# Reordering the matmuls of the last FFN: second products 0 and 1 side by side, wide products 2 and 3 side by side, the output product ahead of the low-rank product

## What is computed

```python
def _L1_ffn_ref(x, U1, V1, b1, U2, V2, b2):      # D_MODEL, D_FF, RANK = 256, 1024, 64
    P = jnp.einsum('bsd,dr->bsr', x, U1)
    H = jax.nn.gelu(jnp.einsum('bsr,rf->bsf', P, V1) + b1)
    Q = jnp.einsum('bsf,fr->bsr', H, U2)
    return jnp.einsum('bsr,rd->bsd', Q, V2) + b2
...
x = x + jnp.tanh(g_ffn[1]) * _L1_ffn_ref(_layernorm(x, axis=-1), ...)
```

## Time and profile before

| | |
|---|---|
| runs before (3) | 698.24, 698.32, 700.71 us, median 698.32 us |
| profiled execution | 698.65 us |
| its span, from first to last instruction | 696.5 us |
| PE busy | 658.6 us (95%) |
| ACT, DVE, POOL busy | 451.7, 427.9, 201.9 us |
| mean granted clock of TensorE | 0.993 |
| bodies of stage d | about 603 to 692 us of the span |

### The profile page before, as it was taken

One profiled execution on the slowest core, in us unless ns is written; L12 is line 12 of the kernel. 1 busy time (PEld: TensorE's weight loads), 2 busy tenths in 40 slices (PEclk: granted clock), 3 DMA queues, 4 the chain that ended last, 5 costly groups with the idle time before them and its releaser, 6 DMA issues.

```text
span 696.5 us, 11909 instructions
## 1 busy us (share of the span) xinstructions
PE 658.6 (95%) x3653; PEld 457.5 (66%) x3653; DVE 427.9 (61%) x981; ACT 451.7 (65%) x1204; POOL 201.9 (29%) x299
## 2 busy tenths in 40 slices
PE   5799899999999999799999999999999998799997
PEld 3565555555544457688888887888888875556654
DVE  7854757776775647566767576566665685343522
ACT  7656655535545543667887787778778877646452
POOL 6565423310110003224432342333223230142110
PEclk9999999999999999999999999999999999999999
DMA  8731116601000005434344443433444331001112
GB/s 280 224 106 61 51 41 233 106 1 61 1 0 1 0 1 123 93 95 101 93 115 123 124 104 88 116 95 93 117 122 121 92 69 25 2 1 61 43 50 90
DMA packets 45809, 57.90 MB, mean 83 GB/s; under 512 B 13152, under 2 KB 24258, under 8 KB 45634
## 3 DMA queue, kind: packets, MB, share of 16 engines
q1 hardware_dynamic: 45762, 57.33, 30.5%
HBM read 27.46 MB, written 4.19 MB: 45 GB/s over the span
## 4 chain that ended last, share of the span: by engine, by line
PE 82%; SPq 5%; ACT 3%; DVE 3%; issue 2%; POOL 2%; DMA 2%; DVEq 0%; POOLq 0%; ACTq 0%
PE bank L1191 12%; PE bank L1493 7%; PE bank L1405 7%; PE bank L1423 6%; PE bank L1203 6%; PE bank L1446 5%; PE bank L1469 4%; PE bank L1636 4%; PE bank L1486 4%; SPq L531 4%; PE bank L1432 4%; PE bank L1167 3%; PE bank L1626 3%; PE bank L1171 2%; PE bank L1627 2%
## 5 line engine op out<-in xcount | busy, mean ns | idle before, releaser
L970 ACT ACTIVATE c_junk<-bank,c_nmx 128x256 bf16<-128x256 f32 x256 | 116.3, 469 | 9.3 <-DVE c_nmx L1961 9.2
L1961 DVE TENSOR_REDUCE c_nmx<-bank 128x4 f32<-128x1024 f32 x64 | 75.3, 1219 | 34.8 <-PE bank L1446 34.8
L1191 PE MATMUL bank<-b_o,cw 128*128 128x512 f32 x192 | 90.8, 603 | 0.2 <-ACT b_o L827 0.2
L803 ACT ACTIVATE b_h<-bank,cb 128x512 f32<-128x512 f32 x48 | 32.8, 686 | 51.2 <-PE bank L1191 51.2
L1090 ACT ACTIVATE d_h<-bank,b_col 128x512 f32<-128x512 f32 x64 | 39.6, 686 | 39.4 <-PE bank L1627 39.4
L992 ACT ACTIVATE c_pT<-bank 128x1024 f32<-128x1024 f32 x64 | 62.0, 1017 | 4.8 <-PE bank L1469 3.7
L1405 PE MATMUL bank<-c_ctxT,wsrcT 128*128 128x256 f32 x256 | 61.8, 386 | 0.0
L1191 PEld LDWEIGHTS bank<-b_o,cw 128*128 128x128 f32 x192 | 34.2, 190 | 41.3 <-issue 39.2
L1423 PE MATMUL bank<-wsrcT,c_ctxT 128*128 128x256 f32 x240 | 56.7, 379 | 0.0
L1469 PE MATMUL bank<-c_stack 99*128 99x256 f32 x256 | 46.7, 315 | 6.6 <-DMA c_stack<-c_rows 6.4
L1405 PEld LDWEIGHTS bank<-c_ctxT,wsrcT 128*128 128x128 f32 x256 | 48.3, 193 | 6.3
(11 more groups left out here) (202 smaller groups left out, 1384.2 us busy)
## 6 DMA issues: line engine op xcount, KB each, us to landing
c_stack<-c_parts SPq DMA_DIRECT2D x192, 128.0 KB
a_ctx<-in_ctx SPq DMA_DIRECT2D x16, 512.0 KB, 4.0
c_ctx<-in_ctx SPq DMA_DIRECT2D x16, 512.0 KB, 3.3
out_x<-x_sb SPq DMA_DIRECT2D x7, 512.0 KB, 2.9
x_sb<-in_x SPq DMA_DIRECT2D x3, 1024.0 KB, 10.2
mask_b<-in_mask_BxS_fk SPq DMA_DIRECT2D x1, 2048.0 KB, 12.8
x_sb<-in_x SPq DMA_DIRECT2D x2, 512.0 KB, 5.5
wsrc_raw<-in_L_xattn_W_src SPq DMA_DIRECT2D x1, 1024.0 KB, 7.3
```

The lines of the kernel that those rows point to most:

```text
L970: op = nc.scalar.activation(c_junk[:, tc, j, :], scores(tc)[:, j, :], ACT.Exp, bias=c_nmx[hg][:, tc, j:j + 1], accum_out=c_sum[hg][:, tc, ...
L1191: op = mm(bank[2 * u + h][:], cw1[:, c, h * P:(h + 1) * P], b_o[n % LANES][:, c, :], start=c == 0, stop=c == DK - 1)
L1961: v.tensor_reduce(c_nmx[hg][:, tc, :], scores(tc), AXIS.X, ALU.max, negate=True)\
```

## The change

On PE, `body_d` runs `second_d(n, 1)` right after `second_d(n, 0)`, so that `hidden_d(n, 2)` and `hidden_d(n, 3)` stand together, and `out_d(n - 1)` stands ahead of `lowrank_d(n + LEAD)`. `out_d` gets one more wait, for the copies of the turned group out of bank 5, which it overwrites. No other engine's program changes, and no instruction is added or taken away.

```diff
@@ out_d
                 need(pe, d_q_ok, n + 1)
+                need(pe, d_xT_ok, 2 * min(n + LEAD + 2, NG))
                 need(pe, d_y_ok, 2 * n)
@@ body_d
                 second_d(n, 0)
+                second_d(n, 1)
                 hidden_d(n, 2)
-                second_d(n, 1)
                 hidden_d(n, 3)
+                if n > 0:
+                    out_d(n - 1, 1 - n % 2)
                 if n + LEAD < NG:
                     lowrank_d(n + LEAD)
-                if n > 0:
-                    out_d(n - 1, 1 - n % 2)
                 second_d(n, 2)
                 second_d(n, 3)
```

## The result

| | before | changed |
|---|---|---|
| median of 20 runs | 698.44 us | 700.83 us |
| lowest and highest | 695.72, 701.48 | 698.32, 703.67 |
| ratio | | 1.0028, 95% interval 1.0015 to 1.0041 |
| turn of body 0 to last output product, from the traces | 85.99 us | 88.12 us |

The change makes the kernel 0.28% slower. The last row of the table isolates the changed part: it is the distance between two starts on PE, the turn of body 0 (605.27 before, 608.54 after) and the output product of group 7 (691.26 and 696.66). It grew by 2.13 us; 0.28% of 698.44 is 2.0 us.

What follows compares the result with a forecast made beforehand. PE, 82% of the chain, bounds the kernel, with DVE's equal 6.00 us path next. Late turns add 2.35 us by body 6, bodies 6 and 7 return 0.28: 698.32 + 2.07 = 700.4 us, range 698.2 to 702.3.

Steps and rivals of the forecast that it cites:

- The price of a form: PE, stage d: entering second products costs 0.14 us, wide products 0.21, once per run; grouping saves 0.35 per body.
- Rival 2: Stage d on PE: form price is paid per half product, so bodies take 12.37 us, about +4.6, 702.9 us; chance 0.06.
- DVE's 6.00 us stay, PE's cover shrinks to 4.79: Low-rank product to next turn: PE stands idle 1.21 us, body 12.02 us against 11.31, 0.71 more.
- Rival 1: Stage d: DVE's path has unseen slack, so the forms' gain comes through; body 10.81 us, 695.5 us; chance 0.08.
- Body 0 gives nothing: Body 0 saves 0.35 us, but POOL's bias additions hold DVE's normalization, so body 1's turn stays at 616.61.
- Rival 3: Body 1: normalization gets ahead of POOL's last addition, turn about 1.3 us earlier; +0.8, 699.1 us; chance 0.06.
- Bodies 6 and 7: No turn there and second 1 waits for the gelu: 9.64 us instead of 9.78, gain 0.14 each, 0.28 together.
- The two paths are equal: Kernel before, low-rank product to next turn: DVE needs 6.00 us and PE has 6.00 us of work.
- The new wait at nothing: Output product's wait for the turned group's copies: taken at nothing, at most 0.06 us in each of 7 places, 0.4 in all.
- The clock unchanged by the idle time: Bodies 2 to 5: granted clock stays 1.00 although PE stands idle 1.2 us in each.

Runs made afterwards that it cites:

- e4: Changed kernel with the low-rank product ahead of the output product again, leaving only the grouping: body 10.93 us, ratio 0.9953 to the kernel before.
- e7: Kernel before with second 0 and 1 and wide 2 and 3 grouped, no swap, DVE normalizing one body earlier: body 10.80 us, ratio 0.9946.
- e3: Changed kernel with DVE normalizing each group one body earlier: body 10.65 us, ratio 0.9909 to the kernel before.
- e1: Changed kernel with DVE taking in the output product before splitting the low-rank product: body 11.11 us, ratio 0.9959 to the kernel before.
- e2: Kernel before, PE untouched, with DVE normalizing each group one body earlier: body 11.16 us, ratio 0.9946 to the kernel before.
- e6: Kernel before with only the output product's new wait added: body 11.31 us, ratio 1.0015 (0.9993 to 1.0037).

## Why the prediction was right

It said 700.4 us and +0.3% (+2.07 us); measured were 700.83 and +0.28%, and +2.13 us in stage d. The near match of the last two is in part luck: from the turn of body 1 to the start of body 6 the loss was 2.25 us instead of 2.35, and bodies 6 and 7 gave back some 0.14 in all instead of 0.28. The two misses cancel; the mechanism does not hang on either.

- The price of a form (0.14 and 0.21 on entering, paid once for a run): right. Second 0 and 1 take 1.88, wide 2 and 3 take 2.03, and e4 gives 0.38 per body where 0.35 was worked out, e7 against e3 0.15 where 0.14 was. Rival 2 (the price is paid per product) is refuted by these. Second products 2 and 3 pay the 0.14 behind the output product too (1.88 for 16), where both sides are fp32 and only the form changes. At the wide products form and precision change together, so what the 0.21 is paid for was not separated.
- DVE's 6.00 us stay, PE's cover shrinks to 4.79: right. The idle time ahead of the turn is 1.15 and the body 12.00 (12.02). e1 and e3 show the cause: both change DVE alone and take the loss away. Rival 1 (slack in the chain) is refuted, since there is no gap between the steps, and its figure of 10.8 us per body needs the chain to be moved, as e3 does.
- Body 0 gives nothing, because of POOL: right, 11.36 us against 11.34. Rival 3 (the normalization gets ahead of POOL's last addition) did not happen: the third addition starts at 616.31 and DVE comes to the normalization at 616.80. That the normalization is held up by POOL was read from its length in every profile, not tried with POOL's additions moved.
- Bodies 6 and 7: the mechanism was right, the size was not. The term was 0.14 us for each; from second 0 to second 0 the changed kernel takes 9.71 us (679.19 to 688.90), against 9.77 before (673.67 to 683.44), a gain of 0.06. The run of second products, with a wait in its middle, took 2.17 us (679.19 to 681.36), close to the upper of the two bounds given (1.14 + 1.01 = 2.15), where 0.07 less was taken. That is 0.15 more than two runs of 1.01, and it eats most of the 0.21 that the wide products save.
- "The two paths are equal": mis-sized by 0.15 us. PE alone would have taken 11.16 us for a body (e2), and DVE's chain set the pace before the change too. It did not touch the sum, which was built on DVE's 6.00 us, but rival 1's price was off by it: 10.65 (e3), not 10.81, with 4.70 from low rank to turn instead of 4.79.
- The new wait at nothing: right (e6). The clock unchanged by the idle time: right, 1.00.

For bodies 6 and 7, timeline of PE in the changed kernel:

```profile
679.19 2.24 PE L1636 MATMUL bank<-d_h,u_sb 128*64 128x256 f32 x16 [0.44 <-ACT d_h L1090]
681.36 0.50 PE L1626 MATMUL bank<-d_pT,v_hi 128*128 128x512 f32 x1
...
684.47 1.95 PE L1636 MATMUL bank<-d_h,u_sb 128*64 128x256 f32 x16
...
688.90 2.24 PE L1636 MATMUL bank<-d_h,u_sb 128*64 128x256 f32 x16 [0.45 <-ACT d_h L1090]
```

The first run lasts 2.24 us where an unbroken one lasts 1.95: the 0.29 us is the wait for the second gelu, and it is inside the row, not in its brackets.

## What to carry to other kernels

Before an operation is moved on the busiest engine, look at what it covers: find the chain on the other engines that starts and ends at that engine, add up what the engine does in between, and take the moved operation out of that sum. An engine that is busy for 42% of a body can still set its pace, if its work lies in one piece between two points of the other. And when a reorder on one engine changes which of two results is ready first, change the order of intake on the other engine with it, or move what closes the chain a whole iteration ahead: here the same PE order loses 0.3% alone, and with DVE's order changed the kernel is 0.4% (e1) or 0.9% (e3) faster than before, 0.5% of the latter from DVE's change by itself (e2).

## What the runs showed of the hardware

A wait of the weight load alone (0.34 us, PE never shown idle) cost 0.13 to 0.15 us in each body: a turn whose first weights were loaded beside the last wide product started 0.23 us behind the start of that product and took 0.97 to the next start, one whose weights were late 0.31 and 1.02.

The granted clock fell to 1.2 GHz (0.50) for some 6.7 us at the end of stage c in the profiled execution of the changed kernel (4 us at 0.50, and 2.7 us to make 0.66 of the next 4), for about as long in e1, and for a shorter time in e6 (0.78 in 598 to 602 us, 0.80 in the next 4); it was 1.00 there in the other six. PE had just stood idle for 1.17 us waiting for a transfer (1.16 in the execution before the change, whose clock did not fall), so that idle time alone does not decide it. What the stretch costs is read from the product that waited for the transfer to the turn of body 0. In the changed kernel and in the kernel before this product is:

```profile
597.84 2.07 PE L1469 MATMUL bank<-c_stack 99*128 99x256 f32 x8 [1.17 <-DMA c_stack<-c_rows]
597.09 1.21 PE L1469 MATMUL bank<-c_stack 99*128 99x256 f32 x8 [1.16 <-DMA c_stack<-c_rows]
```

It is 10.70 us to the turn in the changed kernel (597.84 to 608.54), 8.18 before (597.09 to 605.27), 10.58 in e1, 9.72 in e6 and 8.17 to 8.19 in the other five. So this one stretch, in which PE's program is the same in all nine, makes 1.5 to 2.5 us of difference between single executions.
